# Cross attention's row maxima: a pair of heads makes them half a pair ahead instead of a whole pair

## The reference, cut to what matters

```python
q = (query @ Wq + bq).reshape(b, sq, N_HEAD, KEY_DIM)
k = (key @ Wk + bk).reshape(b, key.shape[1], N_HEAD, KEY_DIM)
v = (value @ Wv + bv).reshape(b, value.shape[1], N_HEAD, VALUE_DIM)
scores = jnp.einsum('bqhd,bkhd->bhqk', q, k) / TEMP
attn = jax.nn.softmax(scores, axis=-1)
out = jnp.einsum('bhqk,bkhd->bqhd', attn, v).reshape(b, sq, N_HEAD * VALUE_DIM)
out = out @ Wo + bo + residual        # then a layer norm, then the FP8 projection
```

## Time and profile before

| | us |
|---|---|
| runs of the kernel | 1927.65, 1911.17, 1922.9 |
| median | 1922.9 |
| span of the profiled execution, first to last instruction | 1916.1 |
| PE / DVE / ACT / POOL busy | 1767.4 / 1270.0 / 920.3 / 940.8 |

### The profile page before, as it was taken

One profiled execution on the slowest core, in us unless ns is written; L12 is line 12 of the kernel. 1 busy time (PEld: TensorE's weight loads), 2 busy tenths in 40 slices (PEclk: granted clock), 3 DMA queues, 4 the chain that ended last, 5 costly groups with the idle time before them and its releaser, 6 DMA issues.

```text
span 1916.1 us, 29762 instructions
## 1 busy us (share of the span) xinstructions
PE 1767.4 (92%) x10698; PEld 885.2 (46%) x10698; DVE 1270.0 (66%) x2503; ACT 920.3 (48%) x1866; POOL 940.8 (49%) x800
## 2 busy tenths in 40 slices
PE   7999989998988999999999999999999999999983
PEld 3544444443444544445545545544554554554431
DVE  5677777777643657756656655665665675667888
ACT  2345676666665243344454444445445444445441
POOL 1000000000001466658888888898888888882111
PEclk9867999999999899999999999999999999999996
DMA  4232113332011000000000000000000000000001
GB/s 115 34 37 35 21 16 36 36 45 55 2 34 55 11 0 1 1 11 4 1 11 4 1 10 4 1 11 1 4 11 1 4 1 1 4 11 23 1 28 38
DMA packets 29129, 34.48 MB, mean 18 GB/s; under 512 B 4290, under 2 KB 27139, under 8 KB 27523
## 3 DMA queue, kind: packets, MB, share of 16 engines
q1 hardware_dynamic: 28984, 32.59, 9.1%
HBM read 14.99 MB, written 4.19 MB: 10 GB/s over the span
## 4 chain that ended last, share of the span: by engine, by line
PE 76%; DVE 16%; ACT 4%; issue 3%; SPq 1%; DMA 1%; POOL 0%; ACTq 0%; DVEq 0%; POOLq 0%
PE psum L974 17%; PE psum L954 14%; PE psum L939 9%; DVE maxima L1247 8%; PE psum L860 8%; PE psum L772 6%; PE psum L810 4%; PE psum L835 4%; PE psum L1005 3%; PE psum L927 3%; PE psum L872 2%; PE psum L986 2%; DVE parts_room L1341 1%; DVE stack_room L1297 1%; ACT stack_room L1116 1%
## 5 line engine op out<-in xcount | busy, mean ns | idle before, releaser
L1247 DVE TENSOR_REDUCE maxima<-psum 128x1 f32<-128x400 f32 (+5 forms) x1664 | 860.1, 580 | 322.7 <-PE psum L939 211.7
L747 POOL TENSOR_TENSOR parts_room<-parts_room,weights_room 128x512 f32<-128x512 f32 (+1 forms) x565 | 706.1, 1283 | 136.3 <-ACT weights_room L1137 136.3
L1137 ACT ACTIVATE weights_room<-psum 128x512 f32<-128x512 f32 (+1 forms) x757 | 405.5, 599 | 491.2 <-PE psum L954 429.4
L1065 ACT ACTIVATE weights_room<-psum 128x512 f32<-128x512 f32 (+3 forms) x640 | 300.2, 535 | 183.4 <-PE psum L835 104.1
L1455 POOL TENSOR_SCALAR rstd<-meanvar 128x2 f32<-128x2 f32 (+1 forms) x24 | 9.8, 408 | 726.9 <-DVE meanvar L1197 726.9
L954 PE MATMUL psum<-stack_room,dk_hi 64*128 64x512 f32 (+1 forms) x1408 | 264.1, 410 | 8.1 <-ACT weights_room L1137 4.8
L939 PE MATMUL psum<-k_later,stack_room 64*128 64x400 f32 (+1 forms) x896 | 243.4, 412 | 22.3 <-DVE stack_room L1297 14.6
L939 PEld LDWEIGHTS psum<-k_later,stack_room 64*128 64x128 f32 x896 | 128.4, 184 | 220.8 <-issue 121.2
L974 PE MATMUL psum<-weights_room,parts_room 128*64 128x512 f32 (+1 forms) x754 | 203.1, 606 | 0.0
L974 PE MATMUL psum<-weights_room,late_room 128*64 128x512 f32 (+1 forms) x760 | 202.5, 605 | 0.0
L835 PE MATMUL psum<-stack_room,stack_room 51*128 51x512 f32 (+3 forms) x640 | 143.4, 448 | 34.2 <-DVE maxima L1247 31.7
(11 more groups left out here) (136 smaller groups left out, 1854.4 us busy)
## 6 DMA issues: line engine op xcount, KB each, us to landing
stack_room<-parts_room SPq DMA_DIRECT2D x84, 128.0 KB
x_block<-x_dram SPq DMA_DIRECT2D x8, 512.0 KB, 4.8
x_middle<-x_block SPq DMA_DIRECT2D x4, 512.0 KB, 3.1
x_block<-x_middle SPq DMA_DIRECT2D x4, 512.0 KB, 3.9
out_dram<-x_block SPq DMA_DIRECT2D x8, 256.0 KB, 2.1
stack_room<-parts_room SPq DMA_DIRECT2D x24, 64.0 KB
parts_room<-ctx_dram SPq DMA_DIRECT2D x1, 1536.0 KB
stack_room<-shift_rows SPq DMA_DIRECT2D x64, 2.0 KB
```

The costliest lines, as they stand in the source:

```text
L747: engine.tensor_tensor(sum_[:kw, :], old[:kw, :], weights[u % NP_WEIGHTS][:kw, :], ALU.add) \
L1065: engine.activation(w_self[s % NW][:, m, 0:n], bank_of(use + m)[:, 0:n], ACT.Exp, scale=SELF_SCALE).then_inc(emptied(use + m), 1)
L1137: engine.activation(weights[u % NP_WEIGHTS][:kw, :], pair_scores[u % NSCORES][:kw, :], ACT.Exp, scale=CROSS_SCALE).then_inc(pair_exp, 1)
L1247: engine.tensor_reduce(maxima[:, p % 2, i // TB, n, i % TB, ch:ch + 1], bank_of(use + n)[:, 0:real - k0], AX.X, ALU.max) \
```

## The change

Beside pair p's second sweep now lie pair p's own maxima of blocks 2 and 3 (in the first half), and pair p + 1's of blocks 0 and 1 (in the second), with the projections for p + 1 between and its value tiles in the first half. Pair 0 has 5 blocks of maxima beside it: its own 1, 2, 3 and two of pair 1. The side lists of its four blocks are now: tiles and own block 1 (16 chunks); own block 2 and the 8 projections; own block 3 and pair 1's block 0 (32 chunks); pair 1's block 1 and its tiles. Block 0's side ends at 0.75 of the block instead of 0.9. Pair 7 has its own blocks 2 and 3 beside its blocks 0 and 1, spread over those 40 slots. In pair 7's blocks 0 and 1, additions and division go to POOL; blocks 2 and 3 keep VectorE.

```diff
-            self.interleave([m for m in main if m[2] == b], side, start=0.0, end=0.9)
+            self.interleave([m for m in main if m[2] == b], side, start=0.0, end=0.9 if b else 0.75)
...
-        sides = [self.pair_tiles(0) + self.pair_sweep1(0, [1]) + self.pair_keys(1) + self.pair_queries(1),
-                 self.pair_sweep1(0, [2]) + self.pair_sweep1(1, [0]), self.pair_sweep1(0, [3]) + self.pair_sweep1(1, [1]),
-                 self.mingled(self.pair_sweep1(1, [2, 3]), self.pair_tiles(1))]
         for p in range(NP):
-            side = []
-            if p == NP - 1:
+            last = p == NP - 1
+            if last:
                 put("tail_weights_load"), put("tail_weights")
-            elif p:
-
-                side = self.pair_keys(p + 1)
-                for b, (queries, tiles) in enumerate(zip(self.pair_queries(p + 1), self.pair_tiles(p + 1))):
-                    side.append(queries)
-                    side += self.mingled(self.pair_sweep1(p + 1, [b]), [tiles])
+
+            own = [self.pair_sweep1(p, [b]) for b in range(NB // 2 if p else 1, NB)]
+            following = [] if last else [self.pair_sweep1(p + 1, [b]) for b in range(NB // 2)]
+            projections = [] if last else self.pair_keys(p + 1) + self.pair_queries(p + 1)
+            tiles = [] if last else self.pair_tiles(p + 1)
+            if p == 0:
+                sides = [self.pair_tiles(0) + own[0], own[1] + projections, own[2] + following[0],
+                         self.mingled(following[1], tiles)]
+            else:
+                side = self.mingled(own[0], tiles[:HT]) + self.mingled(own[1], tiles[HT:TB])
+                side += projections + following[0] + following[1] if following else []
                 side.append((0, lambda p=p: p + 3 < NP and self.put("pair_load", p + 3)))
...
-                self.spread(main, side, range(len(main)))
+                self.spread(main, side, range(len(main) // 2 if last else len(main)))
...
-    def on_vector(p):
-        return p == NP - 1
+    def on_vector(p, b):
+        return p == NP - 1 and b >= NB // 2
```

More of the change, by code:

```diff
@@ L557, in _decoder @@
         for m in range(HP if added_up(p, j) else 0):
-            made[on_vector(p)] += 1
-            added_made[p, b, j, m] = added_on_vector if on_vector(p) else added_on_pool, made[on_vector(p)]
+            made[on_vector(p, b)] += 1
+            added_made[p, b, j, m] = added_on_vector if on_vector(p, b) else added_on_pool, made[on_vector(p, b)]
     def added_with(p, b, j, m):
@@ L1334, in vector_program @@
                 for m in range(HP):
-                    if added_up(p, j) and on_vector(p):
+                    if added_up(p, j) and on_vector(p, b):
                         add(dve, engine, p, b, j, s, m)
@@ L1341, in vector_program @@
                 engine.reciprocal(pair_recip[:, cols], pair_recip[:, cols]).then_inc(inverted, 1)
-            elif kind == "pair_divide" and on_vector(at[0]):
+            elif kind == "pair_divide" and on_vector(*at):
                 n_block = pair_finish_no[at]
@@ L1486, in pool_program @@
                 for m in range(HP):
-                    if added_up(p, j) and not on_vector(p):
+                    if added_up(p, j) and not on_vector(p, b):
                         add(pool, engine, p, b, j, s, m)
-            elif kind == "pair_divide" and not on_vector(at[0]):
+            elif kind == "pair_divide" and not on_vector(*at):
                 n_block = pair_finish_no[at]
```

## The result

| | before | after |
|---|---|---|
| median of 6 runs each (us) | 1925.28 (1911.17 to 1936.14) | 1894.7 (1885.05 to 1908.7) |
| span of the profiled execution | 1916.1 | 1883.9 |
| PE / DVE / ACT / POOL busy | 1767.4 / 1270.0 / 920.3 / 940.8 | 1739.3 / 1245.1 / 919.7 / 986.7 |

The ratio is 0.9851, with a 95% interval of 0.9814 to 0.9889: 1.5% faster.

The account below looks back on a forecast made before the run. TensorE, busy 1767.4 of 1916.1 us, was taken as the bound. The terms -24.8 + 0 + 14.0 + 8.7 + 0 = -2.1 gave 1914.0, scaled to 1920.8; the forecast was 1920, range 1899 to 1937.

Parts of the forecast that it names:

- Pairs 1 to 6: Steady pairs: same pieces in the same slots, another order, so 0 us, bounds -3 and +12; a moved key projection adds 1.9.
- Pair 0: First pair: fewer dense blocks of chunks make it 169.0 us against 195.7, -26.7.
- The wait for the row of shifts: End of pair 0's block 0: block 1's shifts come late, 1.5 us lost before its first scores.
- The last pair, first block: Pair 7's block 0: 30.5 us with its chunks, 7.5 of stall and 2 of clock, 40.0 against 26.0, +14.0.
- The wait for the quantised weights: Start of pair 7: TensorE waits for a bank while VectorE works on the tail's weights, 7.5 us, bounds 0 and 10.
- The clock behind it: Pair 7's first block: after the long wait TensorE runs partly at 1.2 GHz, 2 us, bounds 0 and 5.
- Second block: Pair 7's block 1: chunks, a wait for POOL and a fuller VectorE make 39.0 us against 30.3, +8.7.
- The wait for POOL's division: Pair 7's second block: the first block's division stands behind ten additions on POOL, so TensorE's output projection waits, +1.6 us.
- rival C: Pair 7's first half becomes VectorE's through lock and waits for POOL: 92 us instead of 79, about 1933 in all; chance 0.13.
- A: Start of pair 7: no opening stall, VectorE reaches the chunks in time, -11.6 us, about 1911 in all; chance 0.17.
- B: No opening stall, last two blocks gain 5 us, pair 0's block 2 loses 3 less: -20, about 1901; chance 0.10.
- D: Pairs 1 to 6 each lose 2 us in their short last block to POOL's 32.0 us: about 1932 in all; chance 0.10.

Follow-up runs that it names:

- the run above: Changed kernel with the 16 chunks of pair 1's block 2 moved back beside pair 0's block 3: that block 53.3 us instead of 39.4, pair 1 137.4.
- the lists from step 5: Changed kernel with the last pair's side list over main steps 5 to 39 instead of 0 to 39: median 1894.08 us, ratio to before 0.9874.
- step 9: Changed kernel with the last pair's side list over main steps 9 to 39 instead of 0 to 39: median 1888.31 us, ratio to before 0.9835.
- step 7: Changed kernel with the product of the scales in one-input form and the last pair's side list over main steps 7 to 39: median 1887.66 us, ratio 0.9807.

## Why the prediction was wrong

**Pairs 1 to 6: the step that failed.** I put "the same 64 chunks, 8 projections and 4 tiles in the same 80 slots, in another order" at 0, with bounds of -3 and +12. It was -18.2, or -20.1 with the key projection that moved into pair 1: 20 of the 23 us by which the stages missed the forecast. Three of the budgets of 35, 38, 42 and 32 us for the blocks after the change were close (35.4, 38.3 and 31.7); the third, with the projections in it, came out at 38.6. The fault was to take the 147.4 before as the plain sum of its pieces, which left nothing that an order could win. A check of that sum would have shown it: one of the four key projections has 65 columns and takes 0.66 us, not 1.93, and one value tile takes 0.65. By that the pieces of a pair come to 142.7 (four bare blocks of 26.0, 64 chunks at 0.28, 8 projections, 4 tiles; an estimate), and 4.7 us of 147.4 are none of them. The prices are good to about 1 us a pair: pair 1 with 48 chunks, in the run above, took 137.4 where its pieces come to 138.2. In the views stood four waits for L1297, 2.4 us in all. What the runs showed in place of the 0: a chunk right behind the projection whose queries it reads waits for a trip through two other engines, and moving the projections takes that away, -2.1 us a pair out of the kernel before, +2.1 when two of them are put back into the changed one. The other 1.2 us of the 3.3 a pair stay open, and so do the 1.4 by which 144.1 still lies above the pieces. Pair 6 was also not "alike": it took 145.5 before, one projection less.

**Pair 0:** -30.4 against -26.7. That blocks with 32 chunks lose time was right, confirmed by 13.9 us for 16 chunks put back; the price of 0.28 us for a chunk spread thinly is low for the last 16 of pair 1's 64, whose 6.7 us are 0.42 each. Three of the four blocks came out 1.0 to 1.5 us shorter than I had them: 35.1 for 36.6, 44.9 for 46.0, 39.4 for 40.4; the small projection and tile are part of it. Block 2 kept its 46. The wait for the row of shifts was 1.09 for 1.5. The 3.7 us from transpose to scores in the earlier trace rows were not the row's way, though: TensorE spent them on a value tile (3.61 us at half clock) and waited for nothing. That the 1.5 came near is partly luck.

**The last pair, first block:** +16.3 against +14.0. The wait for the quantised weights came where and as long as predicted, 6.88 us for 7.5, at the second chunk. The clock behind it was mis-sized: I gave 2 us; matmuls ran at half clock until 1695 (granted clock 0.52 from 1684.6 on), 10.4 us of which about 5 are lost (an estimate: the same work at twice the clock). The mechanism was right; 3 us too few for the clock and 0.6 too many for the wait make the 2.3 by which the term was off.

**Second block:** +6.8 against +8.7. The wait for POOL's division was 0.4 and not 1.6. Of the 12 contended pieces (rival C) one showed, 1.85 us for 0.66; POOL's additions had ended before most of the tail's pieces came. C fell for that reason, and because VectorE was busy 56 of 80 us where I had 62 of 79: a reduction of 400 columns close behind another takes 0.50 us (2.01 for four, above) and not the 0.58 of the kernel's mean. "Over 9 tenths busy in the second block" was wrong, it was 27.3 of 37.

**The rivals.** A was wrong on its ground, the opening wait was there. B came nearest in size (-20) for the wrong reason: neither the wait nor the last two blocks gave anything. D had the right place and the wrong sign: POOL was busy in 31.3 of 32 us of the short last block, and TensorE never waited for it.

The rule of the Trainium skill on the shared lock (SBUF — State Buffer, "Who interferes with whom"), as the prediction gives it, didn't bring the 12 us that rival C put on it. The traces agree with it in the 2.8 us inside the opening stretch and in the lists from step 5, step 9 and step 7, each of which met VectorE instructions held beside POOL's additions. By the rule the one that comes second waits until the other's instruction is over; here up to 5.44 us went by, four of POOL's instructions and more, and the measurement decides.

## What to carry to other kernels

Add up the pieces of a steady stage at their own prices, small shapes apart, before you call it full: 4.7 us of 147 were no piece, and a reordering won 3.3 of them by the way, 2.1 by parting four chunks from the projections they waited for. In a hand-written order, keep a consumer several slots behind its producer when the way between them goes through other engines, and spread what one slow engine must drain: 16 chunks cost 6.7 us where they lay thin and 13.9 where they doubled, but 11.6 where every slot was already taken. Ahead of the first piece of a newly placed list, look at what already stands in the draining engine's queue: 9 us of harmless work became a 7 us hole with a half-speed stretch behind it.

## What was unexpected of the hardware

A VectorE instruction that reads two tiles of SBUF can be held back by more than one POOL instruction: the product of two numbers per partition took 4.62, 5.33, 5.44 and 5.44 us in four kernels while POOL's instructions of 1.25 us and more followed one another without a pause, and ended within 0.02 us of POOL's last. In five others beside the same POOL work it took 0.37 to 0.55 us and ended with one of the additions; with a single tile as input 0.20, inside an addition, in both kernels that had it. Which of the two-tile outcomes comes, no run predicts: the changed kernel and the one with the last dense block thinned have the same order there, and took 0.53 and 5.44. On other occasions the two engines alternated (1.63 us for 0.69). A one-input multiply over a whole tile was held too, 3.85 us for 0.43.

The granted clock of an untouched stage differs from execution to execution: 646 to 671 us for the same instructions. One profiled span against another can mislead by 1.3% of this kernel; from where the change begins, pairs with the same pieces agreed within 0.4 us in every run.
